# Attention: the order of row logits, logits and products with v inside a step of TensorE

## The reference

```python
q = (x @ Wq).reshape(b, n, N_HEADS, HEAD_DIM)
k, v = jnp.split(ctx @ Wkv, 2, axis=-1)
...
q = apply_axial_rope(q, pos_map)
k = apply_axial_rope(k, ctx_pos_map)
scale = 1.0 / np.sqrt(HEAD_DIM).astype(np.float32)
logits = jnp.einsum('bqhd,bkhd->bhqk', q, k) * scale
w = jax.nn.softmax(logits, axis=-1)
attn = jnp.einsum('bhqk,bkhd->bqhd', w, v)
...
return attn @ Wout + bout
```

## Time and profile before

| | us |
|---|---|
| median of 3 runs | 1375.43 |
| lowest and highest | 1373.52, 1379.07 |
| the profiled execution: its own time | 1375.91 |
| its span in the trace | 1374.1 |
| cross-attention in it | from 347.0 to about 712 |
| one batch in the loop | 43.74 |

### The profile page before, as it was taken

One profiled execution on the slowest core, in us unless ns is written; L12 is line 12 of the kernel. 1 busy time (PEld: TensorE's weight loads), 2 busy tenths in 40 slices (PEclk: granted clock), 3 DMA queues, 4 the chain that ended last, 5 costly groups with the idle time before them and its releaser, 6 DMA issues. The chain is left out here.

```text
span 1374.1 us, 24202 instructions
## 1 busy us (share of the span) xinstructions
PE 1323.2 (96%) x8482; PEld 1068.6 (78%) x8482; DVE 821.4 (60%) x1494; ACT 486.1 (35%) x764; POOL 520.7 (38%) x371
## 2 busy tenths in 40 slices
PE   8999999998799999999889999999999999999987
PEld 7777778877566677677568788888888899999976
DVE  6776666789687788888744657555521222222238
ACT  4212333344266565666666111111101232233221
POOL 2122222135453344344042018531142786555064
PEclk9999999999799999999999999999999999999999
DMA  8992000002755554455300003240010544452257
GB/s 302 309 322 86 0 0 0 0 8 81 211 175 148 166 159 144 145 163 173 111 2 23 24 24 145 84 150 23 24 39 1 196 146 143 149 204 83 85 164 243
DMA packets 85076, 159.85 MB, mean 116 GB/s; under 512 B 8616, under 2 KB 61992, under 8 KB 81576
## 3 DMA queue, kind: packets, MB, share of 16 engines
q1 hardware_dynamic: 78728, 124.19, 28.7%
q0 software_dynamic: 6272, 34.61, 7.1%
HBM read 109.22 MB, written 69.47 MB: 130 GB/s over the span
## 5 line engine op out<-in xcount | busy, mean ns | idle before, releaser
L1621 ACT ACTIVATE b_pf<-b_rt,b_zero 128x1024 f32<-128x1024 f32 x128 | 142.7, 1115 | 118.4 <-PE b_rt L1259 117.9
L1461 DVE TENSOR_REDUCE b_mx<-b_rt 128x4 f32<-128x1024 f32 x128 | 156.4, 1222 | 41.6 <-PE b_rt L1245 40.9
L2177 DVE SCALAR_TENSOR_TENSOR residual<-c_yp,c_shared,residual 128x512 f32<-128x512 f32 x128 | 92.3, 745 | 103.7 <-PE c_yp L43 95.5
L41 PE MATMUL c_fc<-c_xh,c_w 128*128 128x512 f32 x348 | 136.0, 391 | 0.0
L43 PE MATMUL c_fc<-c_xh,c_w 128*128 128x512 f32 x348 | 135.5, 389 | 0.0
L42 PE MATMUL c_fc<-c_xl,c_w 128*128 128x512 f32 x348 | 135.4, 389 | 0.0
L2343 ACT ACTIVATE c_s<-c_fc 128x512 f32<-128x512 f32 x43 | 25.8, 599 | 228.2 <-PE c_fc L43 228.1
L2191 DVE TENSOR_TENSOR c_hTl<-c_eh,c_hTh 128x384 fp32r<-128x384 f32 x39 | 21.8, 558 | 140.9 <-ACT c_hTh L2367 130.3
L41 PE MATMUL c_fc<-c_ring,c_xTl 128*128 x312 | 105.3, 337 | 0.3 <-issue 0.3
L43 PE MATMUL c_fc<-c_ring,c_xTh 128*128 x312 | 100.4, 322 | 0.0
L42 PE MATMUL c_fc<-c_ring,c_xTh 128*128 x312 | 100.3, 322 | 0.0
(11 more groups left out here) (454 smaller groups left out, 3489.4 us busy)
## 6 DMA issues: line engine op xcount, KB each, us to landing
weights_b<-b_pack SPq DMA_DIRECT2D x124, 200.0 KB
c_eraw<-in_c_we POOLq DMA_DIRECT2D x8, 2176.0 KB, 9.4
b_pack<-b_hi SPq DMA_DIRECT2D x56, 256.0 KB, 2.5
c_rows_in<-in_b_ctx SPq DMA_DIRECT2D x39, 256.0 KB, 10.1
c_rows_out<-in_b_ctx SPq DMA_DIRECT2D x39, 256.0 KB, 10.2
c_xe<-c_rows_in SPq DMA_DIRECT2D x39, 256.0 KB, 2.7
c_rows_out<-c_ye SPq DMA_DIRECT2D x39, 256.0 KB
c_wraw<-in_c_ws SPq DMA_DIRECT2D x11, 768.0 KB, 4.3
```

The lines of the kernel that those rows point to most:

```text
L41: nc.tensor.matmul(out, ll, rh, start=start, stop=False)
L1461: nc.vector.tensor_reduce(out=mx[:, :, 2 * p:2 * p + 2].rearrange("p t e -> p e t"), in_=rt[:, row_bank(g, p):row_bank(g, p) + 2, :].rearr ...
L1621: nc.scalar.activation(pf[:, s:s + 2, :], rt[:, 2:4, :], ACT.Exp, scale=XD ** -0.5, bias=zero[:, :]).then_inc(e_done, 1)
L2177: nc.vector.scalar_tensor_tensor(out=X[:, t, :], in0=yp[:, (n * 4 + k) % 3, :], scalar=shared[:, t:t + 1], in1=X[:, t, :], op0=ALU.mult, o ...
```

## The change

The parts of PE's step are put in another order. The wait for `mt_done`, which stood after `turn_maxima`, goes to the front of the step, since it has to stand before `values`. Nothing else is changed: the same instructions on every engine, and the code of ACT, DVE, POOL and SP is as it was.

```diff
             def body(b, live):
                 for i in range(T):
+                    for k in range(4):
+                        for d in due(i, live, 4 * k + 5):
+                            pe.wait_ge(mt_done, (b + d) * 4 + (k + 1))
+                    for d, q in quads(i, live, LAGV):
+                        values(b + d, q)
+                    for d, p in pairs(i, live, LAGS):
+                        logits(b + d, p)
                     for d, p in pairs(i, live, 0):
                         rows(b + d, p)
                     if isinstance(b, int) and b == 0 and i < 2:
                         use(0, "v", 1, (i,))
-                    for d, p in pairs(i, live, LAGS):
-                        logits(b + d, p)
                     for d, q in quads(i, live, LAGV + 1):
                         turn_values(b + d, q)
                     for k in range(4):
                         for d in due(i, live, 4 * k + 4):
                             if not (fresh(b + d) and k == 0):
                                 turn_maxima(b + d, k)
-                        for d in due(i, live, 4 * k + 5):
-                            pe.wait_ge(mt_done, (b + d) * 4 + (k + 1))
...
-                    for d, q in quads(i, live, LAGV):
-                        values(b + d, q)
                     for step, what, n, parts in PLAN:
```

## The result

The changed kernel takes a median of 1398.32 us (four runs, 1392.68 to 1398.99), the kernel before 1376.47 (1373.52 to 1379.07). The ratio is 1.0144, with a 95% interval from 1.0111 to 1.0177. The forecast was 1386.5 with a range of 1379.5 to 1394. The sign was right, the size was half of what came: +10.6 us in the sum, +22.4 between the two profiled executions (spans of 1374.1 and 1396.5).

The account below looks back on a forecast made before the run. PE, 96% busy, was taken to set the pace. 8.4 + 4.0 + 0.2 + 1.0 - 1.6 - 0.6 - 0.8 = +10.6, rounded to +11 on 1375.9, less 0.5 against the median: 1386.5 us, range 1379.5 to 1394.

Parts of the forecast that it names:

- The loops of 1.73 and 1.71: Odd steps: loops through DVE's maxima (1.73 us) and ACT's exponentials (1.71) exceed PE's 1.57, stalling short-PLAN steps 0.15 each.
- I had 0.9: Step 4 of each loop batch: the second x transpose tile waits 0.9 us for DVE to read the k projection's bank.
- the wait was to be 0.4: Step 12 of each loop batch: the PLAN waits 0.4 us for the first o tile's bank, through ACT and DVE.
- the gain of 0.7: Loop batches: row logits' waits go, 0.48 us in step 5 and shorter ones, 0.7 taken off per batch.
- 4.67 against 3.65: Filling and draining, empty PLAN with transposed maxima: products with v wait for ACT's copy, +1.0 us per pair, four times.
- The pairs of the second kind: Filling and draining, empty PLAN without transposes of the maxima: 3.76 us per pair, +0.1 each, +0.2 for two.
- Rival C: Worse: waits of steps 4 and 12 delay the maxima's transposes and chunks, the clock falls again; about 1396 us, chance 0.10.
- The sum had -0.8: Clock behind 668: a shorter chunk wait might avoid the fall worth up to 1.7 us; half taken, -0.8.
- the loop's 1.4: Batches 1 to 6: net loss of 1.4 us each from stalls and waits less the row logits' gain, +8.4 in all.
- less 0.6: Batch 1: a chunk wait of 0.6 us is covered, since row logits come later; -0.6.
- 1.6 for the chunk: Batch 7: the wait of 1.59 us for the chunk landing at 668 is hidden by longer steps 1 to 8; -1.6.
- +1.0 was taken for a worse order: Batch 8, where exponentials bound: a worse order of the parts costs +1.0 us.

## Why the prediction was wrong, point by point

**Right.** PE is the bound, and nothing is added. The distances alternate between 1.72 and 3.5 to 4.6, and the odd steps stall on ScalarE: the logits at 549.94 have 0.17 of idle time ended by `pf`.

```profile
549.94 0.51 PE L1259 MATMUL b_rt<-weights_b 50*128 50x256 f32 x4 [0.17 <-ACT b_pf L1622]
```

The loops of 1.73 and 1.71 were worked out from starts and lengths of before, and the short distances came at 1.72. In step 4 the second x tile waits for DVE's read of the bank:

```profile
540.79 0.66 PE L1302 MATMUL b_gm<-identity,b_xn 128*128 128x128 f32 x4 [0.48 <-DVE b_bs L1452]
```

I had 0.9; it is 0.48 by the trace, and 0.6 by the starts of the two tiles, which lie 1.11 apart where 0.51 is the first one's own. The pair of steps 4 and 5 loses 0.29 in all, the pair of steps 12 and 13 0.28 where the wait was to be 0.4. These two terms were oversized, and so was the gain of 0.7; together they nearly cancel: 1.56 per batch without the collision, against 1.4. In batch 7 the chunk of q and k is no longer waited for, and the products with v wait for the copy of the maxima, as foreseen: 0.51 and 0.52 by the trace. The cost of that, 4.67 against 3.65 for a pair of steps, came out where the clock is full: with the PLAN in odd steps, the pairs of steps 4 and 8 of batch 7 take 4.68 and 4.67 in the new order and 3.65 each in the old one. The pairs of the second kind take 3.95 there, where 3.76 was forecast from a 2.04 that no row in the prediction gives.

**Missing: the port, +4.3 us.** No step of the prediction asked what DVE's small instructions meet on GpSimd. The claim that row logits and `nm` come earlier in odd steps was in it; the next question, beside what, was not. The row that would have told was in the trace of before (369.06, 1.07 us for 16 elements, six times its usual length). Rival C had a push of `turn_maxima`, but by the waits of steps 4 and 12 and for 0.3 per batch.

**Wrong in sign: the clock.** The sum had -0.8, since the one long wait at 668 goes. It did go, and the clock fell at 679 instead and stayed low for 17 of the next 20 us: +4.4 us in batch 7 against the kernel before, so this term was off by 5.2. In the whole program the two profiled executions have mean clocks of 0.991 and 0.985, which is 5.4 us by the slope. At the clock of before the changed kernel would have taken some 1393 us, just inside the range: that the result lies outside hangs on the clock, that it lies above the forecast on the port and the undersized stalls as well.

Part of this is the luck of the two executions. The 34 runs of the kernel before that stand beside the experiments have a mean clock of 0.9894, the eight runs of the changed kernel one of 0.9870; by the slope that is 2.2 us.

The chance of it was in rival C, at 0.10, with "one more fall like that costs 1.7, three of them 5"; its 1396 was 2 us from the result, in part by luck: its other 4 us were to come from a chunk waited for again in batch 7, which it isn't, and from 0.3 a batch in the loop, of which 0.16 is seen (1.56 against 1.4). The port's 4.3 stand in their place. I had priced a fall by the shortest one in the trace. Batch 0 had a longer one in that same trace (17.1 us, from 345.2 in the clock's records), whose windows I didn't use.

**Undersized: the filling and the draining.** Batches 0 and 1 lost 5.7 us where 2.9 stood: two waits for the copy of the maxima (2.0), one of the second kind (0.1), the loop's 1.4 for batch 1, less 0.6. The trace has one of the two waits as costed:

```profile
383.95 1.07 PE L1272 MATMUL b_av<-b_pf,b_vp 128*32 128x256 f32 x16 [0.91 <-ACT b_mT L1611]
```

The pair of steps 12 and 13 of batch 0 lost 1.24, the pair of 14 and 15 0.9, where 0.1 stood. The remainder stands at steps 4 to 7, which lost 2.7; there the clock is at its lower level in both kernels, and comes back 6 us later in the one after (368.5 against 362.2 in the clock's records). The second profile of the changed kernel separates the two: its batch 0 had 17.0 us at the lower clock, as the kernel before had 17.1, and took 44.47 us against 41.00. So 3.5 of the 4.2 us of batch 0 are stalls of the order and some 0.7 the clock's.

Batch 7 stood at +0.5 without the clock (2.1 for stalls, less 1.6 for the chunk), and lost 2.9. Its steps 0 to 3 lost 1.2 of that, for which the sum had nothing, and its last distance, a long even step without its short partner, 1.1.

**Oversized: batch 8.** +1.0 was taken for a worse order there, and the stretch behind the last row logits was 0.6 shorter. In part this is where the stretch is cut, since batch 7 ends on that long step.

Together, for the two profiled executions:

| stretch | forecast | measured | the difference |
|---|---|---|---|
| batches 0 and 1 | +2.9 | +5.7 | stalls, and some 0.7 by the clock |
| batches 2 to 6 | +7.0 | +11.3 | the port, +4.3; stalls +0.8 and a chunk wait -0.7 cancel |
| batch 7 | -0.3 | +7.3 | the clock, +5.2; stalls +2.4 |
| the rest of the attention | +1.0 | -0.6 | oversized |
| before and behind the attention | 0 | -1.3 | not touched by the change |
| sum | +10.6 | +22.4 | |

**What stays open.** Why the clock falls where it does. Before the fall at 679, PE was busy 9.33 of 11 us (above). In the kernel with the PLAN in odd steps it was busy 7.32 of 10 from 670 to 680, and 7.54 of the next 10, and the clock stayed:

```profile
670.00:680.00 10.00, 7.32 (x90) 4.41 (x82) 6.96 (x13) 5.54 (x8) 0.00 (x0) 1.00 0.66 196
680.00:690.00 10.00, 7.54 (x84) 5.07 (x85) 7.39 (x12) 6.60 (x10) 1.89 (x1) 1.00 0.33 84
```

So the busy time of such a stretch does not tell it. Two executions of the same kernel fall in different places (batch 1 above), which suggests that the place also hangs on something that the order doesn't set. Nor is the new order shown to be what makes the falls in batch 7 long. One profile each had 3.4, 10.2 and 13.7 us at the lower clock there with the products with v in their old place (the kernel before, the new order in the loop alone, logits ahead), and 17.0, 23.9 and 10.2 in the new order (the kernel after, the same again, the new order outside the loop), but 0 in the new order with the PLAN in odd steps. No version that beats both kernels was found; logits ahead of row logits is as good as the kernel before.

## What to carry to other kernels

A step moved on the busiest engine moves the instructions of all the others: for each small DVE instruction that PE waits for, look at what GpSimd does at its new time and at how soon PE needs the result, and search the trace of before for rows of the same line that are several times their usual length. A table that spreads work over steps is tuned for the order in a step, so change both or neither. Where a kernel fills or drains with PE half waiting, give the clock a range and not a point: the same kernel differed by 2.3 us in one batch, and price a fall by the longest of the trace.

## What the runs showed of the hardware

- A DVE instruction of 16 elements per partition took 1.21 us instead of 0.18 beside a GpSimd subtraction of 1.27 us that began 0.09 us earlier, in each of five batches. In the run where GpSimd waits for the negation, its 1.29 us at 553.95 stand beside DVE's maximum over PSUM, which keeps its usual 1.23:

```profile
553.89 1.23 DVE L1462 TENSOR_REDUCE b_mx<-b_rt 128x4 f32<-128x1024 f32 x1
```

- The same collision stands in each batch of the loop of the kernel with logits ahead of row logits, and PE lists no wait there: 43.55 us a batch.
- A fall of TensorE's clock to 1.2 GHz cost about a third of the time that it lasted (2.3 us for 6.8 in batch 1; 0.66 us of span per us of (1 - clock) x span over eight runs of the changed kernel).
- A batch with more work was shorter: 48 more transposes in batch 7 (36 in the odd steps, 12 in the even ones), and 39.67 us instead of 42.06, with the clock at 0.96 instead of 0.80; one profile.
- Runs of the changed kernel at a mean clock of 0.983, 0.987 and 0.993 had spans of 1400.1, 1394.9 to 1395.7 and 1390.9. Even the last is 16.8 us above the profiled execution of the kernel before, so the clock's fluctuation is a part of the loss and not the whole.
